# Eleven of 784 gathered tiles brought row by row by SyncE, in a graph-attention kernel on one Trainium2 core

## The chip, the cores and the metric

One core of a Trainium2 chip runs the whole program. Its engines run their own instruction streams and meet in semaphores: TensorE (PE in the profile; its weight loads are PEld), VectorE (DVE), ScalarE (ACT), GpSimd (POOL) and SyncE (SP), which computes nothing and issues DMAs. The metric is the device time of one execution in microseconds (us), the median of a few runs; lower is better.

## The reference

A graph of 3125 nodes and 100,000 edges, sorted by destination, each edge of one of 5 types r. Each edge scores the product of its destination's query and its source's key, per head (8 heads of 16), a softmax runs over the edges of one type into one node, and the values are summed with these weights; then a projection and two layer norms.

```python
for r in range(R):
    mask = edge_types == r
    q = jnp.einsum('eh,khd->ekd', x_dst, W_Q[r])
    k = jnp.einsum('eh,khd->ekd', x_src, W_K[r])
    v = jnp.einsum('eh,khd->ekd', x_src, W_V[r])
    logits = (q * k).sum(-1) / scale + attn_bias[r][None, :]
    ...
    attn = exp_l / (sum_exp[dst] + 1e-12)
    out = out + jax.ops.segment_sum(attn[:, :, None] * v, dst, num_segments=n)
out = out.reshape(n, HIDDEN)
out = out @ out_proj_w.T + out_proj_b
h = out + node_embeddings
mu = h.mean(-1, keepdims=True)
var = ((h - mu) ** 2).mean(-1, keepdims=True)
return (h - mu) / jnp.sqrt(var + LN_EPS) * ln_gamma + ln_beta
...
x = _layernorm(x + _L0_gnn_ref(x, edge_index, edge_type_5, ...), axis=-1)
```

## The kernel before

**Setup**, some 70 us. TensorE makes keys and values of each node and type, ScalarE copies them out of PSUM, SyncE stores them as a table in memory (`KVtab`: one row of 256 floats, 1 KB, for each node and type). VectorE works out each edge's row number (`kvi`) and the masks of equal neighbours. A flag then chooses between a general way, which is not taken with these inputs, and the fast way (`sync_fast`, `vector_fast` and so on).

**The loop.** The edges are cut into 784 tiles of 128 edges; four tiles are a quad, 196 quads. The program runs 210 steps, one quad entering at each; each engine goes through the steps in the order in which they are written, and waits only for semaphores. In step s:

- GpSimd (`gpsimd_fast`) issues four indirect DMAs (L1374) for each quad in turn, which gather the key and value rows of its 512 edges into `ring`, a ring of 15 quads (and two slots of its own for quads 1 and 2). Before a quad's gathers it waits for the expansion of the queries of three quads before (`q_expanded`), and for the ring slot.
- SyncE (`sync_fast`) issues in this order: the destination keys of quad s + 3 to all partitions (`load_keys`, L655, into `rkb`); the query window of quad s + 2, 128 rows of a table from an address in a register (`load_q`, L667, into `qwin`; a load of 8 registers, L531, for every 8 quads); in some steps a block of x (`load_x`, L674; `xs`, L719); in every third step three DMAs of masks (`load_masks`, L683, waiting for `full_sum`, which VectorE's scan L1161 gives); every seventh step a block of made queries back to memory (L709); and the finished outputs (L727). `load_q` waits for the expansion of quad s.
- ScalarE makes one-hot matrices out of the keys (L791, L795), and the exponentials of the softmax.
- TensorE expands the queries of quad s + 1 with the one-hot matrices and the window (L1464, into PSUM); it needs the window, and the product of the quad two before, whose PSUM bank it reuses. It also turns the scores (L1479), spreads the weights (L1501) and sums the weighted values (L1510).
- VectorE multiplies expanded queries and gathered keys of quad s (L1170, 128 x 512), sums them by head (L1192), runs the scans of the softmax over the edges (L1254, L1269, L1293, L1161; one group of three quads at a time), weights the values of the quad of ten steps before (L1225, 128 x 512) and adds sums to the nodes (L1127).

The wait of the product for its keys, and the gathers, in the code:

```python
e.wait_ge(q_expanded, s + 1)                        # VectorE, before L1170
e.wait_ge(kv_in[s % 6], 64 * (s // 6 + 1))
...
for j in range(4):                                  # GpSimd, L1374
    e.indirect_dma_start(
        kv[:, home(m), j, :], None, KV,
        bass.IndirectOffsetOnAxis(kvi[:, 4 * q + j:4 * q + j + 1], 0)).then_inc(kv_in[m % 6], 16)
```

Of the kernel before, what the change touches and what calls it, by code (L numbers as in the profile page):

```python
# [5 lines left out]
N = 3125  # L6
# [120 lines left out]
def counts(steps):  # L127
# [12 lines left out]
    ("kvi", 1), ("keyf", 1), ("reln", 1), ("pen0", 1), ("pen1", 1), ("pen2", 1), ("sel", 1), ("pen", 1),  # L140
# [154 lines left out]
def build(nc, x_t, x_b, w_kv, w_q, w_o, params, edges, natural, firsts, out):  # L295
    ctx = ExitStack()
    with ctx:
# [21 lines left out]
        pool = sb("pool", [128, POOL])  # L319
        wq = sb("wq", [128, R, C])  # L320
# [3 lines left out]
        keyf = sb("keyf", [128, NT])  # L324
# [41 lines left out]
        first = temp.take([NQP], I32)  # L366
        n0f = temp.take([NQP])
# [45 lines left out]
        stq = room.take([2, R, QW])  # L413
        room = Region(pool[:, :])
# [26 lines left out]
        av = sb("av", [128, AR, 4 * C])  # L441
        rkb = sb("rkb", [128, 3, 512], BF16)
# [16 lines left out]
        nat_in, typ_in, first_in, edges_in = sem("nat_in"), sem("typ_in"), sem("first_in"), sem("edges_in")  # L459
        xT_in, xb_in, clamp_in = sems("xT_in", len(PIECES)), sems("xb_in", len(X_IN)), sem("clamp_in")  # L460
# [19 lines left out]
        kv_in = sems("kv_in", 6)  # L480
        rk_in, keys_dist, onehot = sems("rk_in", 3), sem("keys_dist"), sem("onehot")
# [103 lines left out]
        def sync_setup(e):  # L585
# [3 lines left out]
            e.dma_start(first[:, :], firsts.partition_broadcast(128)).then_inc(first_in, 16)  # L589
            for g in range(G):  # L590
                e.dma_start(clamp[g * R * H:(g + 1) * R * H, :],
                            params[0:R * H].rearrange("(p c) -> p c", c=1)).then_inc(clamp_in, 16)
# [53 lines left out]
        def sync_fast(e):  # L646
            kq = [e.alloc_register(f"kq{m}") for m in range(8)]

# [26 lines left out]

            def load_masks(i):
# [14 lines left out]

            for m in range(3):
                load_keys(m)
# [10 lines left out]
            for s in range(plan.steps):  # L704
# [8 lines left out]
                if s + 2 < NQ:  # L713
                    load_q(s + 2)
                if s % QSTEPS == 0 and 1 <= n and n + 1 < len(LATER_Q):
# [166 lines left out]
        def vector_setup(e):  # L882
# [41 lines left out]
            e.scalar_tensor_tensor(kvi[:, :], est[:, 1, 0:NT], 5.0, est[:, 2, 0:NT], ALU.mult, ALU.add).then_inc(vset, 1)  # L924
            e.scalar_tensor_tensor(keyf[:, :], est[:, 0, 0:NT], 5.0, est[:, 2, 0:NT], ALU.mult, ALU.add).then_inc(vset, 1)
# [183 lines left out]
        def vector_fast(e):  # L1109
            n0 = [e.alloc_register(f"n0{m}") for m in range(8)]  # L1110

            for s in range(plan.steps):
# [52 lines left out]
                if s < NQ:  # L1165
                    e.wait_ge(q_expanded, s + 1)
                    e.wait_ge(kv_in[s % 6], 64 * (s // 6 + 1))
                    if s >= 1:
                        e.wait_ge(logit, s)
                    e.tensor_tensor(  # L1170
# [463 lines left out]
```

## Time and profile before

| | us |
|---|---|
| median of 3 runs | 1132.37 |
| lowest and highest | 1130.26, 1133.01 |
| the profiled execution | 1132.2 |
| its span, first to last instruction | 1130.5 |

Busy of that span: TensorE 912.4 us (81%), VectorE 996.1 (88%), ScalarE 533.0 (47%), GpSimd 759.0 (67%). The granted clock of TensorE was 0.55 of full speed as a mean over the span. How to read it: a view of lines gives the busy time of all instructions that one line of the code issued, the mean of one, and what ended the idle time before them. A view of waits gives for each instruction what released it. SPq is SyncE's queue; its DMA issues and register instructions aren't counted as busy, but each has a duration in the trace, the time in which the queue is held. "issue" is time in which an engine waited for nothing that the profile shows. A DMA's duration on SPq is that of its issue, not of its data.

### The profile page before, as it was taken

The numbers are of one execution on the slowest core, as the hardware profiler recorded it, in microseconds if no ns is written. First come the engines' busy times: TensorE is split into PE (matmuls) and PEld (weight loads), VectorE is DVE, ScalarE is ACT, GpSimd is POOL, SyncE is SP. The second block draws the span as 40 slices with busy tenths as digits, with TensorE's granted clock in tenths as the row PEclk, the third lists the DMA queues.
The fourth block names the chain that finished last, engine by engine and source line by source line (L and its number), as shares of the span: only waits on it lengthen the run. The fifth ranks groups of instructions, "written<-read, shape, count | busy, mean of one in ns | idle before, by whom it ended". The sixth has DMA issues, their size and how long they took to land.

```text
span 1130.5 us, 19008 instructions
## 1 busy us (share of the span) xinstructions
PE 912.4 (81%) x5176; PEld 813.6 (72%) x5176; DVE 996.1 (88%) x1867; ACT 533.0 (47%) x977; POOL 759.0 (67%) x844
## 2 busy tenths in 40 slices
PE   6954587798889888878898977888978788887675
PEld 3523477797778787767787867788877678876665
DVE  4456798998899998999999999999989999999976
ACT  4644444555445554444554454555544344444311
POOL 0047777777777777777777777777777777777500
PEclk9976655555555555555555565556555555555555
DMA  9977667666666666656666666666676566655400
GB/s 301 368 274 220 190 207 201 181 188 191 178 191 192 174 197 192 192 169 184 193 194 190 171 186 188 192 192 181 184 198 175 144 188 174 177 175 157 139 1 13
DMA packets 120945, 209.27 MB, mean 185 GB/s; under 512 B 22797, under 2 KB 79498, under 8 KB 120606
## 3 DMA queue, kind: packets, MB, share of 16 engines
q0 software_dynamic: 37632, 102.81, 31.9%
q1 hardware_dynamic: 82194, 102.94, 29.9%
q10 hardware_dynamic: 1008, 2.25, 0.7%
q8 instruction: 45, 0.74, 0.3%
q14 instruction: 66, 0.54, 0.1%
HBM read 176.92 MB, written 30.99 MB: 184 GB/s over the span
## 4 chain that ended last, share of the span: by engine, by line
PE 34%; DVE 30%; issue 20%; DMA 7%; ACT 5%; DVEq 2%; SPq 1%; POOL 1%; ACTq 0%; POOLq 0%
PE pp L1510 10%; PE pp L1464 9%; PE pp L1501 5%; DVE pool L1254 4%; DVE av L1225 4%; DVE pool L1170 4%; DVE Tt L1161 3%; DMA qwin<-Qfast 3%; PE pp L1527 3%; PE pp L517 3%; DVE LW L1192 2%; PE LT L1479 2%; ACT pool L791 2%; DVE Mt L1269 2%; DVE pool L1150 2%
## 5 line engine op out<-in xcount | busy, mean ns | idle before, releaser
L1374 POOL DMA_INDIRECT ring<-KVtab,kvi x784 | 756.2, 965 | 305.7 <-issue 222.4
L1464 PE MATMUL pp<-qwin,pool 128*128 128x128 bf16 x2352 | 278.6, 305 | 156.2 <-ACT pool L795 85.0
L1464 PEld LDWEIGHTS pp<-qwin,pool 128*128 128x128 bf16 x2352 | 245.4, 146 | 202.9 <-ACT pool L795 111.8
L1510 PEld LDWEIGHTS pp<-ohn,av 128*128 128x128 f32 x1568 | 348.4, 326 | 32.8 <-DVE aggT L1127 32.0
L1510 PE MATMUL pp<-ohn,av 128*128 128x32 f32 x1568 | 354.0, 390 | 20.6 <-DVE aggT L1127 19.4
L1170 DVE TENSOR_TENSOR pool<-pp,ring 128x512 f32<-128x512 f32 x196 | 132.9, 678 | 41.4 <-issue 25.5
L1501 PEld LDWEIGHTS pp<-sel,pool 120*128 120x128 f32 (+1 forms) x536 | 130.3, 325 | 27.8 <-issue 26.1
L795 ACT ACTIVATE pool<-pool,one 128x512 bf16<-128x512 bf16 x196 | 141.4, 722 | 6.4
L813 ACT ACTIVATE Et<-pool 120x512 f32<-120x512 f32 (+1 forms) x66 | 41.7, 631 | 216.0 <-DVE pool L1150 216.0
L1501 PE MATMUL pp<-sel,pool 120*128 120x24 f32 (+1 forms) x536 | 130.1, 392 | 16.6 <-DVE av L1225 15.4
L791 ACT ACTIVATE pool<-rkb,npid 128x512 bf16<-128x512 bf16 x196 | 138.9, 709 | 7.9 <-PE LT L517 6.2
L1225 DVE TENSOR_TENSOR av<-ring,pp 128x512 f32<-128x512 f32 x198 | 133.6, 677 | 2.5 <-PE pp L1501 2.2
L1192 DVE TENSOR_REDUCE LW<-pool 128x32 f32<-128x512 f32 x196 | 132.8, 677 | 0.3
L829 ACT ACTIVATE Tt<-Tt,tiny 120x512 f32<-120x512 f32 (+1 forms) x66 | 47.7, 722 | 149.5 <-DVE Tt L1161 149.5
L806 ACT ACTIVATE pool<-pp 128x512 bf16<-128x512 f32 (+1 forms) x126 | 53.8, 427 | 107.6 <-PE pp L1527 70.9
L1254 DVE TENSOR_TENSOR_SCAN pool<-mk,pool,LT 120x512 f32<-120x512 bf16 x66 | 83.1, 1259 | 4.4 <-PE LT L1479 4.2
L1269 DVE TENSOR_TENSOR_SCAN Mt<-LT,pool 120x576 f32<-120x576 bf16 (+1 forms) x63 | 83.5, 1325 | 2.2
L1161 DVE TENSOR_TENSOR_SCAN Tt<-LT,pool 120x576 f32<-120x576 bf16 (+1 forms) x63 | 83.3, 1323 | 0.1
L1293 DVE TENSOR_TENSOR_SCAN pool<-LT,pool,Et 120x512 f32<-120x512 bf16 x63 | 80.3, 1275 | 0.0
L1479 PE MATMUL LT<-ident,LM 128*120 128x128 f32 (+1 forms) x268 | 69.2, 412 | 0.0
L837 ACT ACTIVATE pool<-Yt 120x512 f32<-120x512 f32 (+2 forms) x82 | 43.1, 544 | 44.1 <-DVE Yt L1240 44.1
L1127 DVE TENSOR_TENSOR aggT<-aggT,pp 128x32 f32 x196 | 34.1, 174 | 28.2 <-PE pp L1510 13.8
(121 smaller groups left out, 789.1 us busy)
## 6 DMA issues: line engine op xcount, KB each, us to landing
rkb<-Ktab SPq DMA_DIRECT2D x196, 128.0 KB
mk<-Mtab SPq DMA_DIRECT2D x201, 100.2 KB
qwin<-Qfast SPq DMA_DIRECT2D x196, 96.0 KB
KVtab<-pool SPq DMA_DIRECT2D x25, 640.0 KB, 5.3
ring<-KVtab,kvi POOLq DMA_INDIRECT x784
Qfast<-pool SPq DMA_DIRECT2D x21, 480.0 KB, 3.5
Qfast<-ring SPq DMA_DIRECT2D x4, 480.0 KB, 7.1
xs<-in_x_b SPq DMA_DIRECT2D x5, 320.0 KB, 4.6
```

The source lines that it names most:

```text
L791: e.activation(ab[:, :], rkb[:, m % 3, :], ACT.Abs, bias=npid[:, 0:1]).then_inc(keys_dist, 1)
L795: e.activation(ohr[:, m % OR, :], ab[:, :], ACT.Relu, bias=one[:, 0:1], scale=-1.0).then_inc(onehot, 1)
L1161: e.tensor_tensor_scan(Tt[:, a - base:b - base][:, ::-1], total_mask(i, a, b)[:, ::-1], at_ring(Sb, i, a, b, 64)[:, ::-1], 0.0 if k == 0 e ...
L1170: e.tensor_tensor(prod[:, :].rearrange("p (j c) -> p j c", j=4), pp[2 + s % 2][:, :].rearrange("p (j c) -> p j c", j=4), kv[:, home(s), :, ...
L1192: e.tensor_reduce(LW[:, i % 3, :, g, :], prod[:, :].rearrange("p (j h d) -> p j h d", j=4, d=D), AX.X, ALU.add).then_inc(logit, 1)
L1225: e.tensor_tensor(av[:, f % AR, :].rearrange("p (j h d) -> p j h d", j=4, d=D), kv[:, home(f), :, C:2 * C].rearrange("p j (h d) -> p j h d ...
L1254: e.tensor_tensor_scan(at_ring(Fb, i, a, b, 0), mask_at(i, 0, a, b, 0), turned_at(i, a, b), at_ring(Fb, i, a - 1, a, 0) if i or k else LOW ...
L1269: e.tensor_tensor_scan(Mt[:, a - base:b - base][:, ::-1], backward_mask(i, a, b)[:, ::-1], at_ring(Fb, i, a, b, 0)[:, ::-1], LOW if k == 0 ...
L1374: e.indirect_dma_start(kv[:, home(m), j, :], None, KV, bass.IndirectOffsetOnAxis(kvi[:, 4 * q + j:4 * q + j + 1], 0)).then_inc(kv_in[m % 6 ...
L1464: last = e.matmul(pp[2 + m % 2][:, j * C:(j + 1) * C], ohr[:, m % OR, j * C:(j + 1) * C], qwin[:, m % 2, k * C:(k + 1) * C], start=(k == 0 ...
L1501: last = e.matmul(to[0:m, :, j, :], Wb[:, p:p + 4 * m].rearrange("p (n j) -> p n j", j=4)[:, :, j], sel.rearrange("p g h -> p (g h)"), sta ...
L1510: last = e.matmul(to, av[:, f % AR, j * C:(j + 1) * C], ohn[:, f % AR, j, :], start=(j == 0), stop=(j == 3))
```

## The change

In 11 quads (22, 39, 55, 71, 87, 104, 120, 137, 153, 170, 186: `LONE`) the fourth tile is no longer gathered by GpSimd. SyncE fetches its 128 rows one by one, each with a DMA of one row (256 floats) whose address comes from a register, into one of two buffers `lkv`. They are spread over the steps before by `lone_rows`: 8 rows in a step, 4 in a step that also loads x or stores outputs (12 of the 182 steps have 4), behind the step's keys and window; the last rows of a tile are issued four steps before its quad. For 8 rows there is one load of 8 registers from the row numbers `lrow`, which VectorE makes in the setup from one more small input. A third and later tile waits until VectorE is done with its buffer. Before the first keys SyncE now waits for `lrow` and for the stores of the whole table. VectorE's product and weighting of these 11 quads become two operations each, one over `lkv` and one over three tiles of `ring`. `keyf`, which the fast way doesn't use, moves into the ring's space.

```diff
-def build(nc, x_t, x_b, w_kv, w_q, w_o, params, edges, natural, firsts, out):
+def lone_rows(plan):
+    quads, rows, s = [], {}, 1
+    while True:
+        k = len(quads)
+        if k >= 2:
+            s = max(s, quads[k - 2] + 13)
+        at, p = {}, 0
+        while p < 128:
+            n = min(128 - p, 4 if s in plan.norm2 or s in X_IN else 8)
+            at[s] = (k, p, p + n)
+            p += n
+            s += 1
+        if s + 3 >= NQ:
+            return quads, rows
+        rows.update(at)
+        quads.append(s + 3)
+LONE, LONE_ROWS = lone_rows(schedule())
+NL = len(LONE)
+def tiles_of(m):
+    return 3 if m in LONE else 4
+def kv_landed(m):
+    return 16 * sum(tiles_of(k) for k in range(m % 6, m + 1, 6))
+def build(nc, x_t, x_b, w_kv, w_q, w_o, params, edges, natural, firsts, lone, out):
     ctx = ExitStack()
     with ctx:
...
+        keyf = ring[:, (KR + 2) * 8 * C - NT:]
         wq = sb("wq", [128, R, C])
         xs = sb("xs", [128, NB, C])
         aggT = sb("aggT", [128, NB * 128 + 32])
         hb = sb("hb", [128, 10, C])
-        keyf = sb("keyf", [128, NT])
         kvi = sb("kvi", [128, NT], U32)
         reln = sb("reln", [128, NT], BF16)
         pen = sb("pen", [128, NW + 1, 4, G, R], BF16)
...
+        lkv = sb("lkv", [128, 2, 2 * C])
+        lrow = sb("lrow", [NL, 128], I32)
...
+            e.dma_start(lon.rearrange("p k c -> p (k c)"), lone).then_inc(lone_idx, 16)
...
+            def load_rows(k, lo, hi):
+                if lo == 0 and k >= 2:
+                    e.wait_ge(lone_sums, k - 1)
+                    e.wait_ge(lone_weighed, k - 1)
+                for p in range(lo, hi):
+                    if p % 8 == 0:
+                        e.load(lr, lrow[k:k + 1, p:p + 8])
+                    row = e.snap(lr[p % 8], min_val=0, max_val=(N - 1) * R + R - 1)
+                    e.dma_start(lkv[p:p + 1, k % 2, :], KV[bass.ds(row, 1), :]).then_inc(lone_in[k % 2], 16)
...
+            e.wait_ge(vset, VSET["lrow"])
+            table_stored(e)
             for m in range(3):
                 load_keys(m)
...
+                if s in LONE_ROWS:
+                    load_rows(*LONE_ROWS[s])
                 if s % QSTEPS == 0 and 1 <= n and n + 1 < len(LATER_Q):
                     load_x(n + 1)
                 if s in X_IN:
...
+            e.scalar_tensor_tensor(lrow[:, :], lon[:, 0, :], 5.0, lon[:, 1, :], ALU.mult, ALU.add).then_inc(vset, 1)
             e.scalar_tensor_tensor(keyf[:, :], est[:, 0, 0:NT], 5.0, est[:, 2, 0:NT], ALU.mult, ALU.add).then_inc(vset, 1)
...
-                    e.wait_ge(kv_in[s % 6], 64 * (s // 6 + 1))
+                    e.wait_ge(kv_in[s % 6], kv_landed(s))
                     if s >= 1:
                         e.wait_ge(logit, s)
+                    n = tiles_of(s)
+                    if n < 4:
+                        k = LONE.index(s)
+                        e.wait_ge(lone_in[k % 2], 16 * 128 * (k // 2 + 1))
+                        e.tensor_tensor(prod[:, 3 * C:], pp[2 + s % 2][:, 3 * C:], lkv[:, k % 2, 0:C],
+                                        ALU.mult).then_inc(lone_sums, 1)
                     e.tensor_tensor(
-                        prod[:, :].rearrange("p (j c) -> p j c", j=4),
-                        pp[2 + s % 2][:, :].rearrange("p (j c) -> p j c", j=4),
-                        kv[:, home(s), :, 0:C], ALU.mult).then_inc(q_times_k, 1)
+                        prod[:, 0:n * C].rearrange("p (j c) -> p j c", j=n),
+                        pp[2 + s % 2][:, 0:n * C].rearrange("p (j c) -> p j c", j=n),
+                        kv[:, home(s), 0:n, 0:C], ALU.mult).then_inc(q_times_k, 1)
                 if o is not None:
                     e.wait_ge(root_done, 2 * group(o) + 1)
                     e.scalar_tensor_tensor(y, y, mv[:, 0, o % 10, 0:1], gab[:, :], ALU.subtract,
...
+                    if s in LONE:
+                        e.wait_ge(lone_sums, LONE.index(s) + 1)
                     if i >= 3:
                         e.wait_ge(spread_out, i - 2)
                     if i == 3:
...
+                    n = tiles_of(f)
+                    if n < 4:
+                        e.tensor_tensor(
+                            av[:, f % AR, 3 * C:].rearrange("p (h d) -> p h d", d=D),
+                            lkv[:, LONE.index(f) % 2, C:2 * C].rearrange("p (h d) -> p h d", d=D),
+                            bank_of(i)[:, 32 * g + 24:32 * g + 32][:, :, None].broadcast_to([128, H, D]),
+                            ALU.mult).then_inc(lone_weighed, 1)
                     e.tensor_tensor(
-                        av[:, f % AR, :].rearrange("p (j h d) -> p j h d", j=4, d=D),
-                        kv[:, home(f), :, C:2 * C].rearrange("p j (h d) -> p j h d", d=D),
-                        bank_of(i)[:, 32 * g:32 * g + 32].rearrange("p (j h) -> p j h", j=4)[:, :, :, None].broadcast_to(
-                            [128, 4, H, D]), ALU.mult).then_inc(weighed, 1)
+                        av[:, f % AR, 0:n * C].rearrange("p (j h d) -> p j h d", j=n, d=D),
+                        kv[:, home(f), 0:n, C:2 * C].rearrange("p j (h d) -> p j h d", d=D),
+                        bank_of(i)[:, 32 * g:32 * g + 8 * n].rearrange("p (j h) -> p j h", j=n)[:, :, :, None].broadcast_to(
+                            [128, n, H, D]), ALU.mult).then_inc(weighed, 1)
                 if o is not None:
                     e.wait_ge(g1_done, o + 1)
                     e.tensor_tensor(y, y, beb2[:, :], ALU.add).then_inc(g2_done, 1)
...
                 if m >= 6:
-                    e.wait_ge(kv_in[m % 6], 64 * (m // 6))
+                    e.wait_ge(kv_in[m % 6], kv_landed(m - 6))
                 q = quad_of(m)
-                for j in range(4):
+                for j in range(tiles_of(m)):
                     e.indirect_dma_start(
                         kv[:, home(m), j, :], None, KV,
                         bass.IndirectOffsetOnAxis(kvi[:, 4 * q + j:4 * q + j + 1], 0)).then_inc(kv_in[m % 6], 16)
...
+                if f in LONE:
+                    e.wait_ge(lone_weighed, LONE.index(f) + 1)
                 e.wait_ge(nodes, f + 1)
                 for j in range(4):
```

SyncE's queue in the steps 4 and 5, before: window of quad 6, the block of x, then keys and window of step 5.

```order
L532 ISA
L667 DMA qwin<-Qfast 128x384
L719 DMA xs<-in_x_b 128x640
L655 DMA rkb<-Ktab 128x512
L532 ISA
L667 DMA qwin<-Qfast 128x384
```

The same place of the change (the ISA ahead of each DMA is the register instruction):

```order
L710 DMA qwin<-Qfast 128x384
L726 TENSOR_LOAD lrow
L727 ISA
L728 DMA lkv<-KVtab 1x256
L727 ISA
L728 DMA lkv<-KVtab 1x256
L727 ISA
L728 DMA lkv<-KVtab 1x256
L727 ISA
L728 DMA lkv<-KVtab 1x256
L777 DMA xs<-in_x_b 128x640
L698 DMA rkb<-Ktab 128x512
```

Four rows and a load of registers stand between the window of quad 6 and the next step; in most other steps it is eight rows. SyncE's part of the program grows from 758 instructions to 3751.

VectorE in step 22, before: the product, the one-hot of nodes, the sum by head, the weighting.

```order
L1150 SCALAR_TENSOR_TENSOR pool<-Mt,clamp,LT 120x448
L1170 TENSOR_TENSOR pool<-pp,ring 128x512
L1182 TENSOR_TENSOR ohn<-reln,io 128x128
L1192 TENSOR_REDUCE LW<-pool 128x4x8
L1225 TENSOR_TENSOR av<-ring,pp 128x512
```

The same step of the change:

```order
L1210 SCALAR_TENSOR_TENSOR pool<-Mt,clamp,LT 120x448
L1234 TENSOR_TENSOR pool<-pp,lkv 128x128
L1236 TENSOR_TENSOR pool<-pp,ring 128x384
L1248 TENSOR_TENSOR ohn<-reln,io 128x128
L1260 TENSOR_REDUCE LW<-pool 128x4x8
L1300 TENSOR_TENSOR av<-ring,pp 128x512
```

One product has become two; nothing else of the order moved.

## Rows read from the trace of the kernel before

**Rows 1.** The page's busy times: us (share of the span) and instructions.
```profile
PE 912.4 (81%) x5176; PEld 813.6 (72%) x5176; DVE 996.1 (88%) x1867; ACT 533.0 (47%) x977; POOL 759.0 (67%) x844
```

**Rows 2.** Timeline of GpSimd: start us, us, instruction, [idle before].
```profile
69.59 1.10 POOL L1374 DMA_INDIRECT ring<-KVtab,kvi  x1 [65.95 <-DMA KVtab<-pool]
...
181.33 0.95 POOL L1374 DMA_INDIRECT ring<-KVtab,kvi  x1 [0.30 <-issue]
...
1064.64 0.94 POOL L1374 DMA_INDIRECT ring<-KVtab,kvi  x1 [0.30 <-issue]
```

**Rows 3.** Waits of GpSimd, 90 to 1066 us: sum, times, longest.
```profile
POOL ring L1374 <- issue: 218.8, 718, 0.3
```

**Rows 4.** Line L1170 from 193 us on: ns min/median/max; idle before it, us and times.
```profile
L1170 DVE TENSOR_TENSOR pool<-pp,ring x174: 657/680/693, 197.3 to 1073.0; 128x512 f32<-128x512 f32 x174
...
  issue: 11.0, 7
  PE pp L1464: 4.6, 3
  DMA ring<-KVtab,kvi: 2.0, 2
```

**Rows 5.** Timeline of SyncE's DMA issues.
```profile
67.59 1.30 SPq L655 DMA_DIRECT2D rkb<-Ktab  x3
...
82.67 0.36 SPq L667 DMA_DIRECT2D qwin<-Qfast  x1
...
90.77 0.35 SPq L667 DMA_DIRECT2D qwin<-Qfast  x1
...
1005.05 0.37 SPq L667 DMA_DIRECT2D qwin<-Qfast  x1
```

**Rows 6.** Waits of SyncE's queue, 90.7 to 1005 us: sum, times, longest.
```profile
SPq L666 <- PE pp L1464: 252.5, 94, 6.6
SPq L683 <- DVE Tt L1161: 211.7, 57, 7.8
SPq L709 <- ACT pool L806: 114.0, 21, 9.8
SPq L655 <- ACT pool L791: 26.8, 70, 1.9
SPq L727 <- DVE hb L1302: 13.8, 9, 7.9
```

**Rows 7.** SyncE's instructions by line: ns min/median/max, first and last start.
```profile
L532 SPq FUSED_REGOPS  x196: 44/44/64, 82.5 to 1056.8; - x196
...
L667 SPq DMA_DIRECT2D qwin<-Qfast x196: 337/343/1292, 82.7 to 1056.9; - x196
...
L655 SPq DMA_DIRECT2D rkb<-Ktab x196: 319/418/1084, 67.6 to 1052.3; - x196
...
L683 SPq DMA_DIRECT2D mk<-Mtab x201: 273/327/462, 68.9 to 1067.5; - x101
...
L727 SPq DMA_DIRECT2D out<-hb x25: 254/429/453, 515.0 to 1127.6; - x25
...
L591 SPq DMA_DIRECT2D clamp<-in_params x3: 351/367/954, 2.5 to 3.9; - x3
...
L531 SPq TENSOR_LOAD <-kbm x25: 465/687/1692, 81.7 to 1047.4; - x25
```

**Rows 8.** Timeline of SyncE: keys of one quad, then its query window.
```profile
413.46 0.34 SPq L655 DMA_DIRECT2D rkb<-Ktab  x1
414.06 0.37 SPq L667 DMA_DIRECT2D qwin<-Qfast  x1
```

**Rows 9.** Timeline of VectorE: the product of quad 185.
```profile
1018.36 0.67 DVE L1170 TENSOR_TENSOR pool<-pp,ring 128x512 f32<-128x512 f32 x1
```

**Rows 10.** Timeline of TensorE: the first expansion of queries.
```profile
85.63 1.44 PE L1464 MATMUL pp<-qwin,pool 128*128 128x128 bf16 x12 [11.42 <-DMA qwin<-Qfast]
```

**Rows 11.** VectorE by line and shape: busy us, mean ns, idle before.
```profile
L1133 DVE TENSOR_TENSOR hb<-pp,xs 128x128 f32<-128x128 f32 x21 | 6.0, 285 | 0.0
```

More of the change, by code:

```diff
@@ L139 @@
     ("n0f", 1), ("n0m", 3), ("kbm", 1), ("v1", 1), ("v2", 1), ("v3", 1), ("v3r", 1), ("wqs", 1), ("negb", 1),
-    ("kvi", 1), ("keyf", 1), ("reln", 1), ("pen0", 1), ("pen1", 1), ("pen2", 1), ("sel", 1), ("pen", 1),
+    ("kvi", 1), ("lrow", 1), ("keyf", 1), ("reln", 1), ("pen0", 1), ("pen1", 1), ("pen2", 1), ("sel", 1), ("pen", 1),
     ("v6", 1), ("v7", 1), ("v67", 1), ("tot", 1), ("tot1", 1), ("totr", 1), ("flag", 1),
@@ L366, in build @@
         first = temp.take([NQP], I32)
+        lon = temp.take([2, 128], I32, NL)
         n0f = temp.take([NQP])
@@ L413, in build @@
         stq = room.take([2, R, QW])
+        assert room.off <= (KR + 2) * 8 * C - NT
         room = Region(pool[:, :])
@@ L459, in build @@
         nat_in, typ_in, first_in, edges_in = sem("nat_in"), sem("typ_in"), sem("first_in"), sem("edges_in")
+        lone_idx = sem("lone_idx")
         xT_in, xb_in, clamp_in = sems("xT_in", len(PIECES)), sems("xb_in", len(X_IN)), sem("clamp_in")
@@ L480, in build @@
         kv_in = sems("kv_in", 6)
+        lone_in, lone_sums, lone_weighed = sems("lone_in", 2), sem("lone_sums"), sem("lone_weighed")
         rk_in, keys_dist, onehot = sems("rk_in", 3), sem("keys_dist"), sem("onehot")
@@ L647, in sync_fast @@
             kq = [e.alloc_register(f"kq{m}") for m in range(8)]
+            lr = [e.alloc_register(f"lr{m}") for m in range(8)]
             def load_keys(m):
@@ L924, in vector_setup @@
             e.scalar_tensor_tensor(kvi[:, :], est[:, 1, 0:NT], 5.0, est[:, 2, 0:NT], ALU.mult, ALU.add).then_inc(vset, 1)
+            e.wait_ge(lone_idx, 16)
+            e.scalar_tensor_tensor(lrow[:, :], lon[:, 0, :], 5.0, lon[:, 1, :], ALU.mult, ALU.add).then_inc(vset, 1)
             e.scalar_tensor_tensor(keyf[:, :], est[:, 0, 0:NT], 5.0, est[:, 2, 0:NT], ALU.mult, ALU.add).then_inc(vset, 1)
@@ L1595, in quad_rows, with lone_tiles @@
     return rows.reshape(2, HQ, n).transpose(1, 0, 2).reshape(HQ, 2 * n)
+def lone_tiles(a):
+    import numpy as np
+    tiles = edge_tiles(a, 0)
+    return np.stack([tiles[:, 4 * quad_of(m) + 3] for m in LONE])
 def kernel(**inputs):
@@ L1625 @@
         "in_firsts": firsts,
+        "in_lone": np.concatenate([lone_tiles(src), lone_tiles(typ)], axis=1),
     }
```

## The prediction

> **What bounds the kernel now.** I read the page's busy shares and costliest groups first, then the waits of each engine, then stretches of the timeline.
>
> VectorE is busy 88% of the span and GpSimd 67% [rows 1], but GpSimd's gathers start 1.25 us apart, 0.95 us of work and 0.30 us of issue [rows 2], and of its waits from 90 to 1066 us none is longer than that 0.3 us [rows 3]. So GpSimd never stands still: 784 gathers at 1.25 us are 980 us, from 69.6 to 1065 us [rows 2]. A quad costs it 5.0 us. VectorE follows at about the same pace: from 193 us on it stands idle before its product of keys and queries (L1170) 12 times, for 11.0 + 4.6 + 2.0 = 17.6 us [rows 4]. Both are near a bound of 5.0 us per step, and the one who would be given something by the change is VectorE, by at most those 17.6 us.
>
> The change puts its work on SyncE's queue, so SyncE is the third engine to read. From the issue of the query window of quad 3 (90.77 us) to that of quad 185 (1005.05 us) [rows 5] there are 182 steps and 914.3 us. In them SyncE waited 252.5 + 211.7 + 114.0 + 26.8 + 13.8 = 618.8 us [rows 6], which leaves 295 us of work, 1.6 us a step. The same work from its parts: a query window takes 44 + 343 ns for its register instruction and its DMA and some 0.2 us for a semaphore, a move and the gaps, keys 418 ns and a gap of 50, the masks 327 + 45 in each step on average (three DMAs every third step), and the rest (register loads, blocks of x and of queries, outputs) 0.25 us: 1.70 us a step, 309 us in all [rows 7, 8]. I take 309.
>
> **Part by part.** *Rows on SyncE.* 11 tiles of 128 rows are 1408 DMAs of one row each, 4 or 8 in each of the steps 1 to 182. Each one is a register instruction, a move and a DMA, as the query window has them; for each 8 rows there is one load of 8 registers. Nothing in the trace is a DMA of one row. The pieces: from the end of the keys' issue at 413.80 us to the start of the window's at 414.06 are 0.26 us [rows 8]; a short semaphore instruction in them, with its gap, is not there for a row, so I take 0.20 us between two row DMAs (44 ns of them the register instruction [rows 7]). The DMA itself: 343 ns with a register's address and 128 partitions, 327 with 40 partitions, 254 for the one output of 53 partitions, the shortest [rows 7]. From 40 partitions of 4 bytes it still took 351 at least [rows 7], so the bytes do not matter, and no DMA was issued under 254 ns. A row is nearest to the 254: neither 53 nor 1 can be dealt out evenly over the core's 16 DMA engines, as 128 can and 40 in part, and the price falls in this order. I take 0.254 + 0.20 = 0.45 us a row; the ends are 0.54 (343 ns) and, below any row, some unknown smaller price. A register load is 687 ns and a gap of 40: 0.73 us [rows 7].
>
> The Trainium skill's "DMA: Bandwidth & Descriptors" (Why a DMA increments its semaphore by 16) says that a DMA issued by SyncE runs on the largest number of engines up to 16 that divides its outer dimension, one for a count such as 127 partitions. By that rule 53 partitions ran on one engine, which is what would make the 254 ns row the right neighbour for one row; no row here shows the engines themselves.
>
> 1408 x 0.45 = 634 us, 176 loads x 0.73 = 128 us: 762 us are added to a queue that had 619 us to spare. That is the argument. SyncE's work becomes 309 + 762 = 1071 us in a stretch that lasted 914.3, 5.9 us a step against 5.02. Nothing hides it: window s+2 is issued ahead of the rows of step s, and window s+3 stands behind them; the keys and the masks stand behind them too, and TensorE can't expand the queries of a quad, nor VectorE multiply them, before its window is there. The stretch grows by 1071 - 914 = 157 us.
>
> Given back: now the product of quad 185 starts at 1018.36, 13.3 us after its window's issue [rows 5, 9]. When SyncE is late, everybody waits for the window, and the distance is the landing and the product: 2.96 us from the issue at 82.67 to TensorE's start at 85.63, which had waited for just this DMA, 1.44 us of matmuls [rows 5, 10], some 5 us in all. That returns 8 us. After step 182 the queue is as before and 125.4 us follow quad 185's window [rows 5], of which 13.3 are in the account already.
>
> *At the start.* SyncE now waits for the table's stores before it asks for any keys: it started at 67.59 us, and GpSimd, which waits for the same stores, at 69.59 [rows 2, 5]. 2 us later, on a queue whose first window then waits for query blocks. On GpSimd's side it costs 2 us in the case in which GpSimd stays the bound, and in mine it is 2 us too, since the windows' issue starts later. One more small load and a small integer operation in the setup are under 0.5 us and beside TensorE's and ScalarE's work: nothing.
>
> *GpSimd.* 11 gathers fewer, 11 x 1.25 = 13.75 us. In my case worth nothing: GpSimd then waits for expanded queries.
>
> *VectorE.* 22 operations over 128 x 512 become pairs of 128 x 128 and 128 x 384: 0.285 us for the small one [rows 11], 0.285 + (0.680 - 0.285) x 2/3 = 0.548 for the other, 0.83 against 0.680 [rows 4], so 0.15 us each, 3.4 us. In my case they lie in VectorE's idle time. New waits in front of them: the last rows of a tile are issued four steps ahead, some 20 us, so none is late; rows of a third tile wait for a buffer freed 13 steps back, which VectorE releases within 11.
>
> *DMA engines.* 1408 packets of 1 KB more and as many fewer from the gathers: no change in bytes, at most a little longer to land. Nothing, or 1 us.
>
> Sum: 1132.2 (this execution; its span is 1130.5, and the median of the runs, 1132.37, is the same within 0.02%) + 157 - 8 + 2 = 1283. The 0.45 is rounded and the first rows are issued when the queue still has room; I say **1280 us**.
>
> **Rivals.** (1) *The row DMA costs as much as a window's*, 343 ns, 0.54 us a row: 760 + 128 + 309 = 1197 us against 914, +283 - 8 + 2, so about 1409 us. For it: it is a DMA of the same kind, with a register's address. Against: 254 ns exists. Chance 0.20.
>
> (2) *The other side: one row is cheap to issue and SyncE keeps its slack.* The point where it turns: (914 - 309 - 128) / 1408 = 0.34 us a row, so a DMA of 0.14 us or less. Then SyncE is never late, GpSimd ends 13.75 us earlier, and of VectorE's 12 waits those go that come late enough: tile by tile, 1.25 us for each one taken off so far, they give 10 us and not 17.6. Less 3.4 us of split operations and 2 us at the start: 1127 us, between 1119 (13.75 in full, nothing against it) and 1132. Against it stands that of all SyncE's DMAs none is below 254 ns. The skill's same page (Anatomy of one DMA, the table on where 2 us go) gives some 50 ns for a sequencer's dispatch. By that figure a row would be 0.25 us, 352 + 128 us would fit in 619, and this rival would be what comes; each of SyncE's rows contradicts it by a factor of five. Chance 0.13.
>
> (3) *The rows don't gate, they only eat the slack*: the price is near 0.14 us, or waits fall together so that gain and loss cancel: within 0.3% of before, 1129 to 1136 us. Chance 0.03. A price between 0.14 and 0.19 us would end between there and 1175: 0.04.
>
> **How the numbers follow.** Forecast 0.60, rival (1) 0.20, cheap but gating 0.04, no change 0.03, faster 0.13. What a measurement can tell from no change is 0.3%, 3.4 us. Faster 0.13, same 0.03, slower 0.84. The range is 1175 to 1425: below it a row DMA would have to cost under 0.18 us, above it more than the window's 343 ns. It holds the forecast and rival (1), and leaves out 0.2.
>
> **What would show it.** In the changed profile: SyncE's row DMAs at 0.25 us and 0.45 us apart; no waits of SyncE on TensorE or on VectorE's totals up to about 1140 us; TensorE's expansion (L1464 before) waiting for the query window in nearly every step instead of for ScalarE; VectorE's busy share down from 88% to under 80%; GpSimd's gathers with waits of up to a microsecond and more in each quad; steps of 5.9 us until quad 185, then of 5.0 again. Wrong if SyncE still waits some hundreds of us in all, which would say that the price of a row was taken too high.

## The result, and the profile after

| | before | changed |
|---|---|---|
| median of 4 runs, us | 1132.69 | 1287.68 |
| lowest and highest | 1130.26, 1134.37 | 1285.52, 1289.78 |
| profiled execution, us | 1132.2 | 1288.74 |
| its span, us | 1130.5 | 1286.9 |

The ratio is 1.1369, with a 95% interval of 1.1352 to 1.1387: the change costs 155 us. The prediction said 1280 us.

The page of the changed kernel, busy times of the engines, then two of its costliest groups (busy us, mean ns | idle before, releaser), and the DMA issues that are new:

```profile
PE 914.9 (71%) x5176; PEld 822.6 (64%) x5176; DVE 1005.8 (78%) x1890; ACT 541.8 (42%) x977; POOL 746.8 (58%) x833
...
L1449 POOL DMA_INDIRECT ring<-KVtab,kvi x773 | 744.0, 962 | 468.0 <-issue 199.1
L1539 PE MATMUL pp<-qwin,pool 128*128 128x128 bf16 x2352 | 280.1, 307 | 333.6 <-issue 307.6
...
lkv<-KVtab SPq DMA_DIRECT2D x1408, 1.0 KB
```

Beside [rows 1] every engine did nearly the same busy time in a longer span: no engine's work grew by anything like 155 us, and none of the four is busier by share than before. That points to a bound that the busy line does not count. SyncE's waits show it (sum, times, longest), from the first steps to quad 185:

```profile
SPq L698 <- ACT pool L849: 4.3, 15, 0.4
SPq L709 <- DMA Qfast<-pool: 3.8, 1, 3.8
SPq L709 <- PE pp L1539: 2.5, 2, 2.1
SPq L785 <- DVE hb L1377: 0.9, 2, 0.7
SPq L717 <- PE pp L1604: 0.4, 1, 0.4
```

They are 11.9 us in 1077, where [rows 6] had 618.8 in 914. SyncE's queue hardly rests any more. What it does is in its instructions by line (ns min/median/max): the register load, the register instruction, then a move and the DMA of one row:

```profile
L726 SPq TENSOR_LOAD <-lrow x176: 526/726/2188, 91.4 to 1161.4; - x176
...
L727 SPq FUSED_REGOPS  x1408: 44/44/49, 92.0 to 1165.0; - x176
...
L728 SPq MOVE lkv<-KVtab x1408: 29/29/29, 92.1 to 1165.1; - x176
L728 SPq DMA_DIRECT2D lkv<-KVtab x1408: 224/228/554, 92.1 to 1165.1; - x176
```

Two steps of the changed kernel on SyncE's timeline (start us, us):

```profile
464.11 0.42 SPq L698 DMA_DIRECT2D rkb<-Ktab  x1
464.79 0.34 SPq L710 DMA_DIRECT2D qwin<-Qfast  x1
466.11 3.54 SPq L728 DMA_DIRECT2D lkv<-KVtab  x8
469.70 0.36 SPq L698 DMA_DIRECT2D rkb<-Ktab  x1
470.31 0.36 SPq L710 DMA_DIRECT2D qwin<-Qfast  x1
471.60 3.24 SPq L728 DMA_DIRECT2D lkv<-KVtab  x8
```

From one window to the next are 5.52 us here, of which eight rows take 3.54 and the load of registers in front of them most of the 0.98 from 465.13 to 466.11. The second batch of eight gives the pitch of a row, the time from the start of one row's DMA to the start of the next: (3.24 - 0.23) / 7 = 0.43 us. And TensorE waits for exactly these windows. The chain of waits over the same 15 us (start us, us, what):

```profile
464.50 1.65 PE pp L1587 x8
466.15 0.43 PE pp L1607
466.58 1.22 issue
467.79 1.44 PE pp L1539 x12
469.23 1.65 PE pp L1587 x8
470.88 0.43 PE pp L1607
471.31 1.92 issue
473.23 1.44 PE pp L1539 x12
```

The expansion of queries (L1539) starts at 467.79, which is 3.00 us after the window's issue at 464.79, and at 473.23, 2.92 us after the issue at 470.31; a window's DMA took 3.0 us from issue to landing in the median of the 66 windows whose landing the trace has. These two steps are no exception: TensorE stood idle for over 0.2 us before 159 of the 183 expansions of the quads 3 to 185, and the median distance from a window's issue to its expansion (quads 10 to 184) fell from 6.8 us to 3.5. Before the change it stood idle in front of this line less than half as long, and most of that for ScalarE's one-hot matrices:

```profile
L1464 PE MATMUL pp<-qwin,pool 128*128 128x128 bf16 x2352 | 278.6, 305 | 156.2 <-ACT pool L795 85.0
```

The chain files the wait under "issue", time in which nothing in the profile released the engine, and hardly names SyncE: its page puts 58% of the span on PE, 26% on "issue" and 1% on SyncE's queue. A reader who went by the chain's shares would look for a slow TensorE.

The end of the stretch, again SyncE's timeline, and then VectorE's product of quad 185:

```profile
1167.11 0.37 SPq L710 DMA_DIRECT2D qwin<-Qfast  x1
1167.53 0.42 SPq L698 DMA_DIRECT2D rkb<-Ktab  x1
1168.20 0.34 SPq L710 DMA_DIRECT2D qwin<-Qfast  x1
```

```profile
1176.05 0.67 DVE L1236 TENSOR_TENSOR pool<-pp,ring 128x512 f32<-128x512 f32 x1
```

The window of quad 3 was issued at 91.03, that of quad 185 at 1167.11: 1076.1 us for 182 steps, 5.91 each. Once the rows are done, the next window goes out 1.09 us later. Where the 156.4 us between the two spans are:

| us | before [rows 5, 9] | changed | difference | predicted |
|---|---|---|---|---|
| up to the window of quad 3 | 90.77 | 91.03 | +0.3 | +2 |
| to the window of quad 185 | 914.3 | 1076.1 | +161.8 | +157 |
| from there to the end | 125.4 | 119.8 | -5.6 | -8 |

And SyncE's queue in the long stretch, summed from the trace by instruction, each with the gap in front of it:

| us | before | changed | predicted |
|---|---|---|---|
| 1408 rows | | 613 (0.436 each) | 634 (0.45) |
| 176 register loads | | 140 (0.795 each) | 128 (0.73) |
| everything else but waits | 315 (1.73 a step) | 321 (1.76) | 309 (1.70) |
| waits | 599 | 2 | 0 |

A row's 0.436 us are 0.238 us of DMA as a mean, 0.044 of the register instruction, 0.029 of the move, and 0.125 of gaps. (These sums count as a wait only a gap of over 0.2 us in front of an instruction that waits for a semaphore, less an ordinary 50 ns, so the waits come out under the view's 618.8 and 11.9. How the rest splits hangs on this: counted as the view does, everything else but waits is 292 us before and 313 us in the changed kernel.)

### The profile page after: what moved, and what is told of

It is laid out like the page before. It is cut to its first block, busy times and chain, and to the rows that moved or that the text cites. A ratio compares the mean times of both kernels' runs of the same rounds, so it can differ in the third digit from the quotient of the medians.

```text
span 1286.9 us, 23445 instructions
## 1 busy us (share of the span) xinstructions
PE 914.9 (71%) x5176; PEld 822.6 (64%) x5176; DVE 1005.8 (78%) x1890; ACT 541.8 (42%) x977; POOL 746.8 (58%) x833
## 4 chain that ended last, share of the span: by engine, by line
PE 58%; issue 26%; DVE 9%; DMA 3%; ACT 2%; DVEq 1%; SPq 1%; ACTq 0%
PE pp L1587 20%; PE pp L1539 18%; PE pp L1576 8%; PE LT L1554 4%; PE pp L1604 4%; PE pp L558 2%; DMA KVtab<-pool 2%; DVE Tt L1221 1%; PE pp L1607 1%; DVE pool L1329 1%; DVE av L1300 1%; PE pp L1593 1%; DVE LW L1260 1%; ACT pool L853 1%; DVE pool L1236 1%
## 5 line engine op out<-in xcount | busy, mean ns | idle before, releaser
L1449 POOL DMA_INDIRECT ring<-KVtab,kvi x773 | 744.0, 962 | 468.0 <-issue 199.1
L1539 PE MATMUL pp<-qwin,pool 128*128 128x128 bf16 x2352 | 280.1, 307 | 333.6 <-issue 307.6
L1539 PEld LDWEIGHTS pp<-qwin,pool 128*128 128x128 bf16 x2352 | 237.3, 142 | 386.4 <-issue 372.6
L1236 DVE TENSOR_TENSOR pool<-pp,ring 128x512 f32<-128x512 f32 (+1 forms) x196 | 131.5, 671 | 13.5 <-PE pp L1539 9.7
L1300 DVE TENSOR_TENSOR av<-ring,pp 128x512 f32<-128x512 f32 (+1 forms) x198 | 132.2, 670 | 0.2
```

Source lines behind the costliest of these rows:

```text
L1236: e.tensor_tensor(prod[:, 0:n * C].rearrange("p (j c) -> p j c", j=n), pp[2 + s % 2][:, 0:n * C].rearrange("p (j c) -> p j c", j=n), kv[:, ...
L1300: e.tensor_tensor(av[:, f % AR, 0:n * C].rearrange("p (j h d) -> p j h d", j=n, d=D), kv[:, home(f), 0:n, C:2 * C].rearrange("p j (h d) -> ...
L1449: e.indirect_dma_start(kv[:, home(m), j, :], None, KV, bass.IndirectOffsetOnAxis(kvi[:, 4 * q + j:4 * q + j + 1], 0)).then_inc(kv_in[m % 6 ...
L1539: last = e.matmul(pp[2 + m % 2][:, j * C:(j + 1) * C], ohr[:, m % OR, j * C:(j + 1) * C], qwin[:, m % 2, k * C:(k + 1) * C], start=(k == 0 ...
```

## The experiments

My theory: the change is slow because SyncE's queue has no slack left for 0.436 us a row; GpSimd's eleven gathers fewer, VectorE's split operations, the bytes of the rows and the wait at the start matter little. Rivals: the 1408 small DMAs slow other transfers down (traffic); the product or the weighting waits for rows; the new waits and the reordered GpSimd cost something of their own. In all experiments line numbers shift by a few, and the code cuts show only the lines that differ.

Some of the runs were made on chips on which the kernel before takes 1315 to 1329 us and not 1132 to 1134 us (more on them in the last section); every ratio is against the kernel before on the same chip.

| | chip's before | kernel, us | ratio | interval |
|---|---|---|---|---|
| four rows, early wait | 1327.69 | 1340.34 | 1.0096 | 1.0072 to 1.0120 |
| GpSimd gathers all 784 | 1327.69 | 1509.17 | 1.1373 | 1.1353 to 1.1393 |
| one DMA for a tile | 1327.69 | 1324.43 | 0.9969 | 0.9946 to 0.9992 |
| fixed addresses | 1327.69 | 1326.76 | 0.9996 | 0.9977 to 1.0014 |
| four rows, late wait | 1134.02 | 1127.55 | 0.9943 | 0.9923 to 0.9964 |
| six rows, late wait | 1134.02 | 1138.21 | 1.0032 | 1.0019 to 1.0045 |
| one DMA for a tile | 1134.02 | 1124.92 | 0.9927 | 0.9904 to 0.9950 |
| fixed addresses | 1134.02 | 1124.74 | 0.9916 | 0.9894 to 0.9937 |
| four rows, early wait | 1315.15 | 1325.46 | 1.0084 | 1.0052 to 1.0116 |
| five rows, late wait | 1315.15 | 1349.71 | 1.0268 | 1.0230 to 1.0306 |
| registers loaded once a tile | 1315.15 | 1434.05 | 1.0903 | 1.0858 to 1.0948 |
| five rows, late wait | 1329.27 | 1361.05 | 1.0242 | 1.0214 to 1.0270 |

**What the relief of GpSimd is worth: all 784 tiles gathered, rows still issued.** The rows go into `lkv` and are used as in the change; GpSimd gathers the eleven tiles too.

```diff
 def kv_landed(m):
-    return 16 * sum(tiles_of(k) for k in range(m % 6, m + 1, 6))
+    return 64 * (m // 6 + 1)
...
-                for j in range(tiles_of(m)):
+                for j in range(4):
```

> The changed kernel, but GpSimd gathers all 784 tiles as before, on top of SyncE's rows (the fourth tile of the eleven quads is brought twice). Queue time: GpSimd is no bound there, 1287 us as with the change, within 2. Rival: if GpSimd's relief were part of what is left, 13.75 us more, about 1300.

1.1373 against the change's 1.1369: giving the eleven gathers back to GpSimd costs nothing that can be seen. That the two ratios agree to the third digit is partly luck, as they are from the two sorts of chips and a row's price differs there (0.59 us here). What weighs more is that SyncE's waits from 90 to 1380 us sum to 5.8 us in this kernel too, and that GpSimd, with all its gathers, still has time to wait 397 us of the whole span for expanded queries. SyncE's queue is the bound whatever GpSimd has to gather. Its largest waits, then GpSimd's:

```profile
SPq L709 <- DMA Qfast<-pool: 3.2, 1, 3.2
SPq L709 <- PE pp L1539: 2.0, 1, 2.0
```

```profile
POOL ring L1449 <- PE pp L1539: 396.7, 165, 5.8
```

**The rows without their number: one DMA of 128 rows for a tile.** The buffer gets rows 0 to 127 of the table, the wrong ones, in one DMA; all of VectorE's, GpSimd's and SyncE's waits stay, VectorE's for the buffer with one DMA to count and not 128.

```diff
-                for p in range(lo, hi):
-                    if p % 8 == 0:
-                        e.load(lr, lrow[k:k + 1, p:p + 8])
-                    row = e.snap(lr[p % 8], min_val=0, max_val=(N - 1) * R + R - 1)
-                    e.dma_start(lkv[p:p + 1, k % 2, :], KV[bass.ds(row, 1), :]).then_inc(lone_in[k % 2], 16)
+                if lo == 0:
+                    e.dma_start(lkv[:, k % 2, :], KV[0:128, :]).then_inc(lone_in[k % 2], 16)
```

> The relief without its price: each of the eleven tiles is brought by one DMA of 128 rows of the table's start instead of 128 DMAs of its own rows, so the values are other ones (this part of the computation is changed). GpSimd issues 773 gathers and VectorE's split operations stay. Expected from the sum of the cheap case: 10 us of VectorE's waits less 3.4 for the split operations and up to 2 at the start, 1124 to 1130 us. Rival, VectorE is the bound: 1132 to 1136.

> The relief without its price again (eleven tiles by one DMA of 128 rows of the table's start, so this part of the computation is changed), on whichever chip this call gets. On a chip where the kernel before takes 1132 us: 0.992 to 0.997, 1124 to 1129 us; where GpSimd is not close to the bound, as on the first batch's chip, 0.997.

The second of the two runs, 1124.92 us, is what rival (2), the one to the other side, foretold (1127 us, between 1119 and 1132): with the rows gone from the queue all the rest of the change is a gain of 0.73%, about 8 us. The first, on the slower sort of chip, is a gain of 0.31%. SyncE's waits in the second, from 90.8 to 1000 us, are those of [rows 6] again, in their four largest lines:

```profile
SPq L708 <- PE pp L1535: 237.3, 91, 6.8
SPq L733 <- DVE Tt L1217: 212.3, 57, 7.2
SPq L761 <- ACT pool L860: 110.7, 21, 9.6
SPq L697 <- ACT pool L845: 33.3, 77, 1.7
```

Waits for `lkv`, split operations, the lone semaphores and the early wait are all still in it, so together they cost less than the gathers give.

**As many DMAs and bytes, but cheaper to issue: fixed addresses.** 1408 DMAs of one row each, spread as in the change, with row numbers known at build time (again the wrong rows); no register loads and no register instructions.

```diff
-                    if p % 8 == 0:
-                        e.load(lr, lrow[k:k + 1, p:p + 8])
-                    row = e.snap(lr[p % 8], min_val=0, max_val=(N - 1) * R + R - 1)
-                    e.dma_start(lkv[p:p + 1, k % 2, :], KV[bass.ds(row, 1), :]).then_inc(lone_in[k % 2], 16)
+                    row = (k * 128 + p) * 11
+                    e.dma_start(lkv[p:p + 1, k % 2, :], KV[row:row + 1, :]).then_inc(lone_in[k % 2], 16)
```

> The same 1408 DMAs of one row in the same steps, but with addresses fixed when the kernel is built (other rows, so other values; this part of the computation is changed) and no register load, register instruction or move. Queue time: 0.228 + 0.05 = 0.28 us a row, 394 us on 323 of other work, 717 in a stretch of 914, so SyncE keeps 200 us of slack: 1125 to 1135 us. Rival, traffic: the data traffic is unchanged, so 1287 us.

> The 1408 one-row DMAs with fixed addresses again (this part of the computation is changed). Queue time: 717 us of SyncE's work in 914, ratio 0.995 to 1.003, a little above f3's for rows ahead of windows. Rival, traffic: 1.137 as with the change.

This decides against traffic: as many transfers of 1 KB in the same steps, and 0.9916 instead of 1.1369 (0.9996 in the first run, on the slower sort of chip). The gain is a little more than the 0.995 to 1.003 that I expected. What changed is the time in the queue, and with it which rows of the table are fetched: they lie in regular order here. That scattered rows are slower to arrive is not tested by itself, but they held nobody up in the changed kernel: VectorE never stood idle before its product over `lkv` (L1234, 11 times), and a window landed in 3.0 us there, where the one landing that the prediction had read from before took 2.96. SyncE's rows, first as lines and then as a timeline:

```profile
L725 SPq DMA_DIRECT2D lkv<-KVtab x1408: 215/252/553, 91.6 to 996.3; - x176
```

```profile
465.91 0.37 SPq L709 DMA_DIRECT2D qwin<-Qfast  x1
466.32 2.34 SPq L725 DMA_DIRECT2D lkv<-KVtab  x8
```

The DMA instruction itself is not shorter (252 ns against 228), but the pitch is (2.34 - 0.25) / 7 = 0.30 us and there is no load in front. So 427 us of rows instead of 613, and no 140 us of loads: 427 + 310 of other work leave 170 us of waits in 907.8 us, and SyncE keeps slack. The prediction's sum for the turning point, taken without loads, says so: with 309 us of other work (914 - 309) / 1408 = 0.43 us a row would be affordable, and 0.30 is below it.

**The turning point: fewer rows in a step.** With n rows in each step a step of SyncE costs about 1.74 + 0.44 n + 0.8 n/8 us, since there is one register load for 8 rows. Against GpSimd's 5.02 us a step the line is crossed just above six rows: 1.74 + 2.64 + 0.6 = 4.98. Four rows a step bring 5 tiles into the loop, six rows bring 8. To keep the price at the start out of it, the wait for the table's stores goes from before the first keys to before the first rows. The edit of the four rows; with six the line keeps its 4 for the crowded steps and has a 6 in place of the 8:

```diff
-            n = min(128 - p, 4 if s in plan.norm2 or s in X_IN else 8)
+            n = min(128 - p, 4)
...
+                if lo == 0 and k == 0:
+                    e.wait_ge(vset, VSET["lrow"])
+                    table_stored(e)
                 if lo == 0 and k >= 2:
...
-            e.wait_ge(vset, VSET["lrow"])
-            table_stored(e)
             for m in range(3):
                 load_keys(m)
```

> Four rows in a step, five tiles, and SyncE waits for the table's stores only before its first row, not before the first keys. Queue time: 3.9 us of SyncE's work in a step of 5.0; GpSimd saves 5 x 1.25 = 6.25 us, VectorE pays 10 x 0.15 = 1.5: ratio 0.996 to 1.000 of the kernel before. Rival, lateness within a step: two microseconds of rows ahead of each window and of each mask load make TensorE wait here and there though SyncE has slack on average; the first batch's four rows came at 1.010, and then this comes at 1.005 to 1.01.

> Six rows in a step, eight tiles, the table wait late as in f1. Queue time: 6 x 0.436 + 0.75 x 0.795 + 1.77 = 4.98 us a step, right at the 5.02 of the loop: the turning point, ratio 1.00 to 1.02. Were the price of a row's DMA nearer to the window's 0.343, it would be 5.7 us a step and 1.11.

Four rows are faster than before by 0.57% (0.36 to 0.77), 6.5 us, a little more than expected: 5 gathers fewer are 5 x 1.25 = 6.25 us [rows 2]. **This version beats both kernels** and computes all of the reference. Its SyncE, from 90.8 to 1000 us, has waits left (272 us in all, the three largest lines below), and GpSimd, from 90 to 1066 us, still goes from gather to gather with 0.3 us of issue, as in [rows 3]:

```profile
SPq L740 <- DVE Tt L1222: 92.0, 40, 7.0
SPq L766 <- ACT pool L865: 76.2, 21, 6.5
SPq L709 <- PE pp L1540: 75.3, 37, 5.2
```

```profile
POOL ring L1450 <- issue: 217.9, 715, 0.3
POOL ring L1450 <- DVE av L1301: 6.4, 21, 0.3
```

Six rows are slower by 0.32%, 4 us, although GpSimd has 8 gathers fewer. SyncE's waits of [rows 6] are down to 57 us, and GpSimd begins to wait for expanded queries (20.2 us in all, up to 3.3 us at a time, where no wait of [rows 3] was over 0.3). Their largest lines:

```profile
SPq L766 <- ACT pool L865: 21.7, 10, 5.5
SPq L740 <- DVE Tt L1222: 12.7, 5, 4.5
```

```profile
POOL ring L1450 <- PE pp L1540: 20.2, 18, 3.3
```

By the sum above the mean slack on this chip would be used up just above six rows a step; the loss begins at six already. My reading is that a step with masks, queries or outputs is above the mean and that there is little to catch up with. That is argued from the waits and not tested, and seven rows a step were not run.

**The early wait, and five rows.** Four rows with the wait where the change has it, and five rows with the late one.

```diff
-            n = min(128 - p, 4 if s in plan.norm2 or s in X_IN else 8)
+            n = min(128 - p, 4)
```

> Four rows in a step instead of eight, which makes room for five tiles (640 rows) over 160 steps. SyncE's queue time as the bound: 4 rows at 0.436 us and half a register load at 0.795 are 2.1 us, on 1.77 us of its other work, 3.9 us a step against 5.0, so SyncE waits again and the time is 1128 to 1133 us. Rival, traffic: if it were the row DMAs themselves that slow the windows' and keys' landing, 640 of 1408 rows would give 5/11 of the 155 us, about 1200 us.

> f1 with the one difference that SyncE waits for the table's stores before the first keys, as the change does. The prediction's 2 us for this wait, where GpSimd is the bound: f1's ratio of 0.994 plus 0.002, about 0.996. If the wait costs nothing, 0.994; if lateness of rows in a step were what made the first batch's 1.010, that again.

```diff
-            n = min(128 - p, 4 if s in plan.norm2 or s in X_IN else 8)
+            n = min(128 - p, 4 if s in plan.norm2 or s in X_IN else 5)
```

> Five rows in a step, seven tiles, late wait. Queue time: 5 x 0.436 + 0.625 x 0.795 + 1.77 = 4.45 us of a step of 5.0; GpSimd saves 8.75 us against 6.25 with four rows. Slack on average is enough and the ratio is 0.990 to 0.995, as good as f1's or better. Rival, lateness within a step: between four rows (0.994) and six (1.003), 0.998.

> Five rows in a step and seven tiles once more, for a chip on which the kernel before takes 1130 to 1135 us. SyncE's work by the prices of such a chip: 5 x 0.44 + 0.625 x 0.80 + 1.73 = 4.43 us a step of 5.0. If slack on average is what counts, 0.992 to 0.995 of the kernel before, no worse than four rows; if lateness within a step does, 0.998. On a chip with the pauses of the first and third batch, where four rows took 0.84 us each, 1.02 to 1.03.

All four came on chips where before takes 1315 to 1329 us. Four rows: 1.0096 and 1.0084; I had expected a small gain or no change both times and missed. Five rows: 1.0268, a miss as well where a small gain had been expected, and 1.0242, expected for such a chip once the first had been read. The budget of these runs says part of the reason: a row cost SyncE 0.84 us as a mean with four rows, and 0.75 with five in the first of these runs, not 0.44. Four rows and half a load are then 4 x 0.84 + 0.4 = 3.8 us a step and not 2.1; SyncE's waits sum to 48 us in the second run with four rows (from 90 to 1100 us; 40 in the first) and to 4 us in the second with five (from 90 to 1150 us; 8 in the first). The two largest of the second run with four rows ("remote" is a release of which the trace has no instruction), the largest of the second with five:

```profile
SPq L765 <- ACT pool L864: 15.2, 7, 4.8
SPq L709 <- remote: 9.0, 5, 2.9
```

```profile
SPq L709 <- DMA Qfast<-pool: 2.0, 1, 2.0
```

So with five rows the slack is gone, as in the change, at another price of a row. With four rows some slack is left on average and the kernel is slower all the same; why is not settled. What the early wait costs where GpSimd is the bound is not separated by any of them, and five rows on a chip of 1132 us were not measured: both stay open.

**The loads alone.** The change, but registers are loaded once for each tile, so that most rows are the wrong ones; 11 loads in place of 176.

```diff
-                    if p % 8 == 0:
+                    if p == 0:
```

> The change with all its 1408 row DMAs and their register instructions, but the eight registers are loaded once per tile instead of 16 times (so each tile brings eight rows over and over: this part of the computation is changed). If queue time simply adds, 165 loads of 0.795 us, 131 us, are gone from 1076: 945 us for the 182 steps against 914, and 1287 - 131 = 1156, less what slack the faster loop can't use back, ratio 1.02 to 1.03. Rival, the loads hide behind something: 1.13.

1.0903, where 1.02 to 1.03 was expected, a miss; at 0.436 us a row the stretch would have been 614 + 7 + 309 = 930 us. That chip's rows cost 0.629 us each: 885 us of rows, 7 of loads, 313 of the rest and 15 of waits, 1221 us in the stretch. Against the 1.1373 of the kernel with all gathers, on another chip, where rows cost 0.59, the loads taken out are worth 4.7% of 1315, 62 us, where 165 x 0.795 = 131 us were to go; the rows of this run, dearer by 0.04 us each, are 51 us of the difference. It does show that the queue is full with hardly any loads in it; how much the loads are worth on a chip of 1132 us was not measured.

## Why the prediction was right

1280 us were predicted and 1287.68 measured, 0.6% apart. What matters is which steps of the sum held.

- **SyncE's queue becomes the bound.** Held: waits of 11.9 us in place of 618.8, steps of 5.91 us where 5.9 was said. The one-DMA and the fixed-address kernels show it by experiment: the first takes the row DMAs out, the second leaves as many of them and makes them cheaper to issue, all waits and split operations stay, and both end below before.
- **Price of a row, 0.45 us.** 0.436. The DMA was taken as 0.254 from its nearest row [rows 7] and is 0.238 as a mean; between two DMAs 0.20 was taken and 0.198 is there. To go by the shortest DMA in the trace, that of 53 partitions, rather than by the window's 343 ns was right; one row is a little cheaper still. By the Trainium skill's "DMA: Bandwidth & Descriptors" (Why a DMA increments its semaphore by 16) both run on one engine. The trace is in keeping with this: 228 ns against 254, while the 128-row DMA of the one-DMA kernel took 378. That the number of engines sets the price of an issue is an inference from these three, and no run isolates it.
- **A cheap row (rival 2).** Fell. No row DMA took less than 224 ns in the changed kernel. The table of the Trainium skill's "DMA: Bandwidth & Descriptors" (Anatomy of one DMA) has about 50 ns for a sequencer's dispatch, but for DMAs that GpSimd issues, which the prediction left out when it applied the figure to SyncE; by it a row would have been 0.25 us and the kernel faster. The trace has 228 ns, and the measurement decides.
- **Register loads, 0.73 us.** 0.795, 12 us more in all: the mean of the loads is 0.756 and not the 687 ns of the median in [rows 7], since some took up to 2.2 us. The mean of the same 25 loads before, 0.80 us in the trace, would have been the better term, since a sum over many is made of means.
- **The rest, 1.70 us a step.** 1.76, 12 us more in all. Before it was 1.73 by the same sum, 315 us for the 309 taken, so half of the error is in my adding up and half came with the change.
- **The stretch.** +161.8 against +157: -21 for the rows, +12 for the loads, +12 for the rest, +2 of waits. That the sum came so close is partly luck: errors of 21 us and of 24 us stand against each other.
- **Given back, 8 us.** 5.6. The distance from the window of quad 185 to its product was to fall from 13.3 to about 5 us and is 8.9, so this term gave 4.4 us; the other 1.2 are in the last quads, which no step of the prediction had. The landing took what was said in the steps shown above (2.9 to 3.0 us to TensorE's start), but not every engine takes up its part as soon as it is there. The expansion of quad 185 starts 3.92 us after the window's issue, at 1171.04, behind TensorE's other matmuls, and the product another 5.0 us later, behind VectorE's other operations; over the quads 10 to 184 the median distance is 8.9 us. I had counted only the landing and the matmuls.
- **The start, 2 us.** The first keys went out 1.27 us later (68.86, before 67.59) and the first window 1.39 later (84.06, before 82.67), but the window of quad 3 only 0.26 later, because SyncE still stood idle between the windows of quads 2 and 3, for 2.6 us before and 0.6 now, which took the lateness up.
- **GpSimd's relief is worth nothing here.** Held: GpSimd waits 188.2 us for expanded queries in the changed kernel, far more than the 13.75 us of eleven gathers, and still waits in the kernel in which it gathers all 784. That each gather taken off is worth up to 1.25 us while GpSimd is the bound fits too: four rows gave 6.5 us for 6.25, the one-DMA kernel about 8 for 13.75.
- **VectorE's split operations, 0.83 us a pair.** 0.285 and 0.547: 0.83. In the idle time, as said: VectorE's share went from 88% to 78%.
- **The signs.** GpSimd was to wait in each quad; it waited 188.2 us on TensorE's expansion, up to 4.9 us, but only 104 times for 196 quads. TensorE's wait for its window was there, but not under the name that I gave: the profile names the window's DMA in two waits alone and calls 157 others "issue".

These are GpSimd's waits of the changed kernel, from 90 us on, against [rows 3]:

```profile
POOL ring L1449 <- issue: 195.7, 642, 0.3
POOL ring L1449 <- PE pp L1539: 188.2, 104, 4.9
POOL ring L1449 <- DVE av L1300: 13.1, 10, 2.7
```

## What to carry to other kernels

A queue that only issues DMAs has a budget like an engine: add up its instructions with their gaps and loads between two fixed points, and compare with the time of a step, because the busy line does not show it and the chain of waits may call its lateness "issue". Moving gathers from one queue to another can pay while the receiving queue's slack (its waits, here 619 us) covers count x pitch and the loads that go with it (613 + 140 us) with some to spare, and by no more than the relieved engine is really the bound; here four rows a step gained 0.6%, six lost 0.3% and eight lost 14%. With rows cheaper to issue (0.30 us each with addresses known beforehand, or one DMA for a tile) the rest of the same change was a gain of 0.7 to 0.8%, though with the wrong rows.

## What the runs showed of the hardware

- A DMA's cost to SyncE depends little on what it carries: 228 ns for one row of 1 KB, 254 for 53 partitions, 378 for 128 rows of 1 KB (medians, the 254 a single one). A whole tile in one DMA held the queue about as long, 439 ns as a mean with its gap, as one single row with its register instruction, move and gaps (436 ns).
- The register address costs 0.13 us of a row's 0.436 (0.304 without). That the DMA instruction itself was shorter with a register's address (228 ns) than without (252) I had not expected, and no run explains it.
- On some chips the same kernel takes 1315 to 1329 us and not 1132 to 1134. The single instructions have the same medians there (the row DMA 228 ns, the gather 946 to 949 ns, at a mean granted clock of 0.54), but now and then one of SyncE's is held, most often for 0.3 to 0.7 us and up to 1.5. After 90 us of the kernel with all 784 gathers 292 of SyncE's instructions took over 0.3 us more than the median of their kind and 250 gaps of over 0.4 us stand where nothing was waited for (in the changed kernel on a chip of 1132 us 30 and none), while on the other engines the two kernels hardly differ (VectorE 1 and 1, GpSimd 13 and 14). A move of SyncE that takes 29 ns in all of its 1408 instances in the changed kernel took up to 1418 ns in the kernel with all 784 gathers:

```profile
L728 SPq MOVE lkv<-KVtab x1408: 1/29/1418, 94.5 to 1384.2; - x176
```

In the one-DMA kernel on such a chip there were 31 stretches of over 0.4 us after 90 us in which no engine did anything, 38.9 us in all; before and the changed kernel on a chip of 1132 us had none. A row was 0.59 to 0.84 us and not 0.44, and not even one price for a chip: on the same one it was 0.59 with eight rows a step and 0.84 with four. What holds the instructions is not explained by any run here, and the change itself was not run on such a chip. Four rows a step with the late wait were a gain of 0.6% on one chip, and with the early wait a loss of 0.8 to 1.0% on two others; as the wait differs too, how much of this is the chip is open. Five rows with the late wait lost 2.4 to 2.7% on such chips.
